# Small vectors loaded as one array, four token blocks requested first, the first tile's turned tokens copied by ScalarE alone

## The chip, the cores and the metric

The kernel runs on all 8 cores of one Trainium2 chip. Each core takes one of the eight sequences of the batch and works alone, with its own copy of all weights; nothing is exchanged between cores. The metric is device time in microseconds (us), of the slowest core. Engines are TensorE (PE), VectorE (DVE), ScalarE (ACT) and GpSimd (POOL); SyncE (SP) only issues DMAs here. POOL issues DMAs too: SP's travel on queue q1 and POOL's on queue q0, which also convert float32 to bf16 on the way.

## The reference

For `x` of shape (8, 2048, 1024), one layer of four parts, each added to `x` after a layer norm:

```
x = x + attn_a(layernorm(x))   # differential attention with normed q, k, 8 heads of 2 x 64
x = x + ffn(layernorm(x))      # one 1024x1024 matrix rounded to int4, plus a rank-16 term
x = x + attn_b(layernorm(x))   # causal attention with rotary positions, 16 heads of 64
x = x + ffn(layernorm(x))
```

What this case needs is the beginning of `attn_a`:

```
q, k, v = x @ Wq.T, x @ Wk.T, x @ Wv.T
cos_scale = 15 * sigmoid(cos_logit_scale_raw) * (1 + 0.5 * tanh(cos_head_delta - mean))
L1 = l2norm(q1) @ l2norm(k1).T * cos_scale       (L2 likewise from q2, k2)
G  = tanh(delta_gain * (L1 - L2))
lambda = exp(sum(lambda_q1 * lambda_k1)) - exp(sum(lambda_q2 * lambda_k2)) + 0.5
attn = softmax(L1 + G) - lambda * softmax(L2 - G)
y = rmsnorm(attn @ v) * subln_weight * 0.5
```

The small vectors are the four lambda vectors of 64, `cos_head_delta` and `delta_gain` of 8, `subln_weight` of 128, and one number, `cos_logit_scale_raw`.

## The kernel before, in words

Every engine's program is a list, written out in the order of the Python code; an engine runs its list in order and waits where a semaphore is named. A `Slot` counts the DMAs on one semaphore, and its token waits for all that were started on it so far. There is no scheduler for the part in question.

The tokens are 16 blocks of 128 rows, four blocks to a tile of 512. Stage 1 computes Q, K and V for all four tiles, in two pairs. A block b goes through these steps:

- `load_x1(b)` (SP): 512 KB into one of four buffers `x[:, b % 4]`. Block b + 4 is loaded when block b has been applied.
- `ln1_stats(b)`: two BATCH_NORM_STATS (L433) and one aggregate (L439) on DVE, then two tiny POOL operations (L189, L184) that make the reciprocal deviation.
- `ln1_apply(b)` (DVE, L191): the normed block, in bf16, into `wq[:, b % 8]`.
- `turn_pe(1)`: PE turns the block with the identity `c_ident` into two PSUM tiles, `pT0` and `pT1`, four matmuls each; ACT copies `pT0` (L175) and DVE casts `pT1` (L199) into `xn[t % 2]`. A PSUM tile is written again only when its copy is done.

At the beginning POOL issues `c_blk`, `c_ident`, then `w_q` in three pieces (columns 0 to 255, 256 to 511, 512 to 1023), `w_k` and `w_v` in two pieces each, and three small arrays. SP issues blocks 0 and 1 of x, the eight small vectors, each spread over 128 partitions by `bcast` (`wsub` has one number per partition), and blocks 2 and 3. Then the first four blocks are prepared, DVE in the order stats 0, stats 1, apply 0, stats 2, apply 1, stats 3, apply 2, apply 3, and turned.

Behind that DVE and ACT compute the scales of attention A out of the small vectors (`sc`, `gs`, `wsc`, `lam`, `cvec`, `lnc`), with two table loads on ACT. `group_qk` is one group: eight matmuls `pqk<-xn,w_q` of 128x512 for one head of one tile; it needs the four blocks of its tile and its piece of `w_q` (groups 0 and 1 the first, 2 and 3 the second, 4 to 7 the third). ACT squares the result, PE sums over 64 rows with `c_blk` (in `norm_of`, one group late), ACT takes logarithm and exponential, and DVE writes Q. The stage ends in a barrier of all engines; attention A, whose first matmul is `pD<-Qn,K`, begins after it.

Of the kernel before, what the change touches and what calls it, by code (L numbers as in the profile page):

```python
# [11 lines left out]
OP = mybir.AluOpType  # L12
# [8 lines left out]
HA = 8  # L21
HB = 16
LAMBDA_INIT = 0.5
# [163 lines left out]
def ts(q, out, a, s1, op0, s2=None, op1=None):  # L187
    if op1 is None:
        q.add(lambda e: e.tensor_scalar(out, a, s1, None, op0))  # L189
    else:  # L190
        q.add(lambda e: e.tensor_scalar(out, a, s1, s2, op0, op1))  # L191
# [6 lines left out]
def copy(q, out, in_):  # L198
    q.add(lambda e: e.tensor_copy(out, in_))  # L199
# [6 lines left out]
def _ap(t, offset, dims):  # L206
    return bass.AP(t.tensor if isinstance(t, bass.AP) else t, offset, dims)
# [50 lines left out]
def build_program():  # L258
# [3 lines left out]
    g = Prog(nc, base)  # L262
    pe, ve, ac, po, sy = g.all()

    di = {}

    def dram_in(name, shape):
        di[name] = nc.dram_tensor(name, list(shape), F32, kind="ExternalInput").ap()
# [2 lines left out]
    for w in ("WqT", "WkT", "WvT", "WoT", "WqB", "WkB", "WvB", "WoB", "fker"):  # L271
        dram_in(w, (NCH, 128, D))
    dram_in("bo", (D,))
    for w in ("lamq1", "lamk1", "lamq2", "lamk2"):
        dram_in(w, (64,))
    dram_in("dgain", (HA,))
    dram_in("chd", (HA,))
    dram_in("clsr", (1,))
    dram_in("wsub", (128,))
    dram_in("fbias", (D,))  # L280
    dram_in("fa", (NCH, 128, 16))
    dram_in("fb", (16, D))
# [9 lines left out]
    def sb(name, shape, dtype, stack=None):  # L292
        return (stack or base).enter_context(nc.sbuf_tensor(name, list(shape), dtype))
# [41 lines left out]
    wsc = sb("wsc", (128, 1), F32)  # L335
    lam = sb("lam", (128, 1), F32)
    gs = sb("gs", (128, HA), F32)
# [7 lines left out]

    sl_x = [Slot(g, f"d_x{i}") for i in range(4)]
    sl_w = [Slot(g, f"d_w{i}") for i in range(6)]
    sl_c = [Slot(g, f"d_c{i}") for i in range(3)]
    sl_o = Slot(g, "d_o")
    sl_f = Slot(g, "d_f")  # L350
    sl_wq = [Slot(g, f"d_wq{i}") for i in range(2)]
# [6 lines left out]
    W3 = [sb(f"w3_{n}", (128, NCH, D), BF16, s1) for n in "qkv"]  # L358
    blk = sb("c_blk", (128, 128), BF16, s1)
    ident = sb("c_ident", (128, 128), BF16, s1)  # L360
    sl_c[0].start(po, blk[:, :], di["blk"])
    c_tok = sl_c[0].start(po, ident[:, :], di["ident"])
    w_tok = []
    wq1_tok = []
    for k in range(2):
        w1_tok = sl_wq[k].start(po, W3[0][:, :, 256 * k:256 * (k + 1)],
                                w_cols(di["WqT"], 256 * k, 256))
        wq1_tok.append(w1_tok)
    for i, n in enumerate(("WqT", "WkT", "WvT")):
        for hf in range(2):  # L370
            if i == 0 and hf == 0:
                w_tok.append(w1_tok)
                continue
            w_tok.append(sl_w[2 * i + hf].start(
                po, W3[i][:, :, 512 * hf:512 * (hf + 1)], w_cols(di[n], 512 * hf, 512)))
# [3 lines left out]

    sc = sb("sc", (128, 400), F32, s1)  # L380

    def bcast(dst, name, n):
        return sl_c[1].start(sy, dst, _ap(di[name], 0, [[0, 128], [1, n]]))

    x_tok = {}

    def load_x1(b):
# [1 line left out]

    load_x1(0)  # L390
    load_x1(1)
    for i, n in enumerate(("lamq1", "lamk1", "lamq2", "lamk2")):
        bcast(sc[:, 64 * i:64 * (i + 1)], n, 64)
    bcast(sc[:, 256:264], "chd", HA)
    bcast(sc[:, 264:265], "clsr", 1)
    bcast(gs[:, :], "dgain", HA)
    s_tok = sl_c[1].start(sy, wsc[:, 0:1], di["wsub"])
    load_x1(2)
    load_x1(3)

# [73 lines left out]
    def turn_pe(n):  # L474

        for _ in range(n):
            b, a_tok = late_turn.popleft()
            t, tb = b // 4, b % 4
            toks = []
            pe.wait(a_tok)  # L480
            for k, q in enumerate((ac, ve)):
                pe.wait(pT_free[k])
                for c in range(4):
                    col = 128 * (4 * k + c)
                    mm(pe, pT[k][:, 128 * c:128 * (c + 1)], wq[:, b % 8, col:col + 128],
                       ident[:, :], True, True)
                q.wait(pe.done())
                out = xn[t % 2][:, 4 * k:4 * k + 4, 128 * tb:128 * (tb + 1)]
                if q is ac:
                    act(ac, out, blocks_of(pT[k][:, :], 4), AF.Copy)  # L490
                else:
                    copy(ve, out, blocks_of(pT[k][:, :], 4))
                pT_free[k] = q.done()
            xt[b] = (pT_free[0], pT_free[1])

    pqk_free = [None] * QK_BANKS
    pss_free = [None] * 2
# [6 lines left out]
    def norm_of(dst, t, h, bank, bi, p_tok, is_q):  # L504

        nonlocal n_nrm
        i = n_nrm % 2
        n_nrm += 1
        ac.wait(p_tok, sq_free[i])
        act(ac, sqb[i][:, :], bank[:, :], AF.Square)  # L510
        sq_tok = ac.done()

        def rest():
            pe.wait(sq_tok, pss_free[i])
            mm(pe, pss[i][:, :], blk[:, :], sqb[i][:, :], True, True)
            s_tok = pe.done()
            sq_free[i] = s_tok
            ac.wait(s_tok, rn_free[i])
            act(ac, rn[i][:, :], pss[i][:, :], AF.Ln, bias=lntiny)
            pss_free[i] = ac.done()  # L520
            ac.wait(pss_free[i])
            if is_q:
                act(ac, rn[i][:, :], rn[i][:, :], AF.Exp, scale=-0.5, bias=lnc[:, h:h + 1])
            else:
                act(ac, rn[i][:, :], rn[i][:, :], AF.Exp, scale=-0.5)
            ve.wait(ac.done())
            cap = c1e6[:, h:h + 1] if is_q else 1.0 / COS_EPS
            stt(ve, dst[:, h, QT * t:QT * (t + 1)], rn[i][:, :], cap, bank[:, :], OP.min, OP.mult)
            rn_free[i] = pqk_free[bi] = ve.done()

        late.append(rest)
# [107 lines left out]
    ve.add(lambda e: e.reduce_sum(sc[:, 270:271], sc[:, 0:64], AX))  # L639
    ve.add(lambda e: e.reduce_sum(sc[:, 271:272], sc[:, 128:192], AX))  # L640
    ts(ve, sc[:, 272:273], sc[:, 272:273], 1.0 / HA, OP.mult)
    ts(ve, gs[64:128, :], gs[64:128, :], -1.0, OP.mult)
    ts(ve, wsc[:, 0:1], wsc[:, 0:1], (1.0 - LAMBDA_INIT) * math.sqrt(128.0), OP.mult)
    ve.wait(ve.done())
    ts(ve, sc[:, 280:288], sc[:, 256:264], sc[:, 272:273], OP.subtract)
    ac.wait(ve.done())
# [478 lines left out]
    for s in range(-3, NS + NKS):  # L1125
        step_tanh(s + 2)
        step_exp(s)
        u, k = (s - NKS) // NKS, s % NKS
# [53 lines left out]
    pss_free = [y_evac[len(units) - 1]] * 2  # L1182
# [230 lines left out]
    for s in range(-2, NB + 5):  # L1413
        stepb_exp(s)
        stepb_Y(s - 2)
        if 0 <= s - 2 < NB:
            t, c, j = blocks[s - 2]
            if j == 4 * t + 3:
                i = t * (HB // 2) + c
                k = norm_b(t, c, i, s - 2)  # L1420
# [16 lines left out]
def _host_prep(inputs):  # L1437
    f = np.float32

    def rows(w):  # L1440
        return np.ascontiguousarray(w.reshape(NCH, 128, D))

    x = np.asarray(inputs["L0_attn_a_x"], f)
    com = {}
    for k, n in (("WqT", "Wq"), ("WkT", "Wk"), ("WvT", "Wv"), ("WoT", "Wo")):
        com[k] = rows(np.asarray(inputs["L0_attn_a_" + n], f).T)
    com["bo"] = np.asarray(inputs["L0_attn_a_bo"], f)
    com["lamq1"] = np.asarray(inputs["L0_attn_a_lambda_q1"], f)
    com["lamk1"] = np.asarray(inputs["L0_attn_a_lambda_k1"], f)
    com["lamq2"] = np.asarray(inputs["L0_attn_a_lambda_q2"], f)  # L1450
    com["lamk2"] = np.asarray(inputs["L0_attn_a_lambda_k2"], f)
    com["dgain"] = np.asarray(inputs["L0_attn_a_delta_gain"], f)
    com["chd"] = np.asarray(inputs["L0_attn_a_cos_head_delta"], f)
    com["clsr"] = np.asarray(inputs["L0_attn_a_cos_logit_scale_raw"], f).reshape(1)
    com["wsub"] = np.asarray(inputs["L0_attn_a_subln_weight"], f)
    wqkv = np.asarray(inputs["L0_attn_b_W_qkv"], f)
    for i, k in enumerate(("WqB", "WkB", "WvB")):
        com[k] = rows(wqkv[:, D * i:D * (i + 1)])
    com["WoB"] = rows(np.asarray(inputs["L0_attn_b_W_o"], f))
    com["fker"] = rows(np.asarray(inputs["L0_ffn_kernel"], f))  # L1460
    com["fbias"] = np.asarray(inputs["L0_ffn_bias"], f)
    com["fa"] = np.ascontiguousarray(np.asarray(inputs["L0_ffn_a"], f).reshape(8, 128, 16))
    com["fb"] = np.asarray(inputs["L0_ffn_b"], f)

    half = 32
    theta = 1.0 / (10000.0 ** (np.arange(half, dtype=np.float64) / half))
    ang = np.arange(T, dtype=np.float64)[:, None] * theta[None, :]
    cos_ = np.cos(ang).T.astype(f)
    sin_ = np.sin(ang).T.astype(f)
    com["cosb"] = np.ascontiguousarray(np.tile(cos_, (4, 1)))  # L1470
    sin_block = np.concatenate([-sin_, sin_], axis=0)
    com["sinbs"] = np.ascontiguousarray(np.tile(sin_block, (2, 1)))
    com["tri"] = np.ascontiguousarray(np.triu(np.ones((128, 128), f)))
    idx = np.arange(128)
    pm = np.zeros((128, 128), f)
    pm[idx ^ 32, idx] = 1.0
    com["perm"] = pm
    com["ident"] = np.ascontiguousarray(np.eye(128, dtype=f))
    com["blk"] = (idx[:, None] // 64 == idx[None, :] // 64).astype(f)

    in_maps = []
    for i in range(N_CORES):
        m = dict(com)
        m["xN"] = np.ascontiguousarray(x[i])
        in_maps.append(m)
    return in_maps
# [11 lines left out]
```

How the kernel before makes its waits and increments, by code:

```python
    def wait(self, *tokens):  # L57
        for tok in tokens:
            if tok is None:
                continue
            sem, val = tok
            if self.seen.get(sem.name, 0) >= val:
                continue
            self.seen[sem.name] = val
            self.ops.append([lambda e, s=sem, v=val: e.wait_ge(s, v), None, 0])
# [11 lines left out]
    def emit(self, engine):  # L77
        for fn, sem, k in self.ops:
            inst = fn(engine)
            if sem is not None:
                inst.then_inc(sem, k)
```

## Time and profile before

| | |
|---|---|
| runs of the kernel before | 1708.33, 1709.23, 1766.12 us (median 1709.23) |
| the profiled execution | 1708.93 us |
| its spans, first to last instruction | 1699.2 to 1706.4 us, the longest on core 3 |
| granted TensorE clock, mean of a core | 0.960 to 0.966 |
| PE busy (core of the page) | 1497.0 us, 88% |
| ACT busy | 1268.7 us, 74% |
| DVE busy | 1047.3 us, 61% |
| POOL busy | 532.5 us, 31% |
| DMA, mean over the span | 58 GB/s |

The span leaves out some 2.5 us around the first and the last instruction. A row of a timeline reads: start in us, busy time in us, engine, line, operation, output and input tiles, shapes, how many alike; in brackets how long the engine had been idle and what ended that. "SPq" is the SP queue issuing a DMA, and its time is that of the issue, not of the transfer. Merged rows with a count cover all that is alike, with what lies between them on other engines. Buffer numbers are left out of names.

### The profile page before, as it was taken

To read this page: it belongs to the slowest core of one execution; us is meant where nothing else is said; L and a number is where in the kernel's file an instruction comes from. 1 tells how busy PE (TensorE), PEld (TensorE's weight loads), DVE (VectorE), ACT (ScalarE), POOL (GpSimd) and SP (SyncE) were. 2 spreads that over 40 slices of the span, in tenths; PEclk is the share of its full clock that TensorE was granted. 3 is DMA by queue.
4 is the path that set the end of the run, shared out by engine and by line. 5 is a ranking of instruction groups with operands and counts; after the bars stand their busy time and mean duration, and the time that the engine had idled before them with its cause. 6 is when DMAs were issued, how large, how long until landed. Compare 5 with 4: busy or idle time off the path is not lost.

```text
span 1706.1 us, 40220 instructions; the slowest of 8 cores (1699.2 to 1706.4 us)
## 1 busy us (share of the span) xinstructions
PE 1497.0 (88%) x13132; PEld 787.9 (46%) x13344; DVE 1047.3 (61%) x1939; ACT 1268.7 (74%) x1904; POOL 532.5 (31%) x1089
## 2 busy tenths in 40 slices
PE   3899978789999999999999998759998899989987
PEld 1344434455555555555555555324443344444443
DVE  4474468878788787888878788432625454324215
ACT  2666649899999999999999999103234688878990
POOL 3010014444444444554444444522623000001001
PEclk9899989999999999999999999879997799989989
DMA  9614031211101111111111222473005222222303
GB/s 183 120 56 110 35 77 56 82 31 32 56 19 41 41 31 51 18 44 39 32 49 45 68 31 56 78 116 81 1 1 97 40 81 69 66 72 41 101 7 77
DMA packets 131468, 99.54 MB, mean 58 GB/s; under 512 B 99891, under 2 KB 115379, under 8 KB 131270
## 3 DMA queue, kind: packets, MB, share of 16 engines
q1 hardware_dynamic: 113910, 82.10, 18.0%
q0 software_dynamic: 17360, 14.88, 6.4%
q8 instruction: 115, 1.88, 0.5%
q14 instruction: 83, 0.68, 0.1%
HBM read 67.79 MB, written 20.97 MB: 52 GB/s over the span
## 4 chain that ended last, share of the span: by engine, by line
PE 41%; ACT 25%; issue 12%; DVE 5%; DMA 2%; POOL 0%; ACTq 0%; DVEq 0%; SPq 0%; POOLq 0%
ACT E L175 13%; PE pL L164 10%; ACT Gt L175 7%; PE pBb L164 6%; PE pY L171 5%; ACT EB L175 4%; PE pB L164 4%; PE pS L166 4%; PE pYb L171 4%; PE pL L166 3%; PE pD L164 3%; DVE Sx L184 2%; PE pS L164 1%; DMA xn<-xn 1%; PE pY L164 1%
## 5 line engine op out<-in xcount | busy, mean ns | idle before, releaser
L184 DVE TENSOR_TENSOR Sx<-pL,Gt 128x512 f32<-128x512 f32 x768 | 503.2, 685 | 138.3 <-PE pL L963 53.9
L175 ACT ACTIVATE E<-Sx 128x1024 bf16<-128x1024 f32 (+1 forms) x512 | 433.1, 846 | 15.4 <-DVE Sx L184 14.9
L175 ACT ACTIVATE EB<-pS,cst 128x1024 bf16<-128x1024 f32 (+1 forms) x320 | 296.5, 988 | 66.6 <-PE pS L166 63.7
L171 PE MATMUL pY<-V,E 128*128 128x129 bf16 x4096 | 308.2, 221 | 23.9 <-ACT E L175 11.7
L175 ACT ACTIVATE Gt<-pD 128x512 bf16<-128x512 f32 x512 | 306.4, 598 | 24.4 <-PE pD L164 15.4
L171 PEld LDWEIGHTS pY<-V,E 128*128 128x128 bf16 x4096 | 259.7, 98 | 92.7 <-issue 40.3
L166 PE MATMUL pL<-Q,K 64*128 64x256 bf16 x1536 | 198.8, 274 | 23.8 <-ACT E L175 15.8
L164 PE MATMUL pD<-Qn,K 128*128 128x256 bf16 x1024 | 196.4, 273 | 23.1 <-ACT Gt L175 15.8
L189 POOL TENSOR_SCALAR st<-st 128x1 f32<-128x1 f32 x64 | 17.8, 278 | 502.9 <-DVE st L439 486.3
L175 ACT ACTIVATE E<-pL 128x512 bf16<-128x512 f32 x256 | 154.1, 602 | 6.0 <-PE pL L171 0.5
L166 PE MATMUL pS<-Q,K 64*128 64x512 bf16 (+3 forms) x640 | 123.4, 379 | 21.8 <-ACT EB L175 15.7
L171 PE MATMUL pYb<-V,EB 128*128 128x65 bf16 x2176 | 134.3, 202 | 4.7 <-DVE ytb L184 4.5
L175 ACT ACTIVATE qb<-pL 128x512 bf16<-128x512 f32 x64 | 38.2, 597 | 128.0 <-PE pL L164 125.5
L171 PEld LDWEIGHTS pYb<-V,EB 128*128 128x128 bf16 x2176 | 91.6, 101 | 76.8 <-issue 70.6
L166 PEld LDWEIGHTS pL<-Q,K 64*128 64x128 bf16 x1536 | 60.7, 94 | 139.6 <-issue 139.6
L184 POOL TENSOR_TENSOR cu<-Yt,cst 128x2 f32<-128x2 f32 x64 | 44.1, 688 | 228.6 <-DVE Yt L199 228.4
L184 DVE TENSOR_TENSOR EB<-EB,c_tri 128x256 bf16<-128x256 bf16 x128 | 36.5, 290 | 123.7 <-ACT EB L175 122.8
L963 PE MATMUL pL<-Q,K 64*128 64x256 bf16 x512 | 100.2, 276 | 0.0
L164 PEld LDWEIGHTS pD<-Qn,K 128*128 128x128 bf16 x1024 | 75.4, 97 | 45.3 <-issue 39.3
L433 DVE BATCH_NORM_STATS2 st<-x 128x6 f32<-128x512 f32 x128 | 86.3, 685 | 13.8 <-DMA x<-xN 11.2
L164 PE MATMUL pB<-Wo,Q 128*128 128x512 bf16 x240 | 71.7, 384 | 19.0 <-DMA Q<-yt 11.3
L184 DVE TENSOR_TENSOR ro<-pL,x 128x512 f32<-128x512 f32 x64 | 43.6, 682 | 64.6 <-ACT qb L175 64.4
(165 smaller groups left out, 2167.8 us busy)
## 6 DMA issues: line engine op xcount, KB each, us to landing
x<-xN SPq DMA_DIRECT2D x32, 512.0 KB, 5.2
x<-x SPq DMA_DIRECT2D x32, 512.0 KB, 3.3
out<-x SPq DMA_DIRECT2D x16, 512.0 KB, 2.8
x<-fker SPq DMA_DIRECT2D x3, 2048.0 KB
x<-WoT SPq DMA_DIRECT2D x2, 2048.0 KB
xn<-xn SPq DMA_DIRECT2D x16, 256.0 KB, 2.1
w_k<-WkT POOLq DMA_DIRECT2D x2, 1024.0 KB, 40.7
w_v<-WvT POOLq DMA_DIRECT2D x2, 1024.0 KB, 58.2
```

Source lines behind the costliest of these rows:

```text
L164: q.add(lambda e: e.matmul(out, lhsT, rhs, start=start, stop=stop))
L166: q.add(lambda e: e.matmul(out, lhsT, rhs, start=start, stop=stop, tile_position=pos))
L171: q.add(lambda e: e.matmul(out, lhsT, rhs, start=first, stop=last, skip_group_check=True))
L175: q.add(lambda e: e.activation(out, in_, func, **kw))
L184: q.add(lambda e: e.tensor_tensor(out, a, b, op))
L189: q.add(lambda e: e.tensor_scalar(out, a, s1, None, op0))
L433: ve.add(lambda e: e.bn_stats(st[:, b, 6 * half:6 * half + 6], x[:, b % 4, 512 * half:512 * (half + 1)]))
L963: pe.add(lambda e, s=s, cs=cs, js=js, h=h, qsl=qsl, jj=jj: e.matmul(pL[2 * (s % 2) + 1][:, cs], K[64:128, h, js], Q[64:128, h, qsl], start ...
```

## The change

Three edits. The eight small vectors are laid out by the host code as one array `small` of 128 x 329 float32, already repeated over the partitions, and one DMA brings it to `sc`, between blocks 1 and 2 of x. `gs` and `wsc` were loaded directly before; now a DVE copy and the two multiplies that were there fill them from `sc`. `c_blk` moves on POOL from the first place to behind the first two pieces of `w_q`, on a slot of its own, and PE waits for it where it first reads it. For the first four blocks both PSUM tiles of turned tokens are copied by ACT.

```diff
-    for w in ("lamq1", "lamk1", "lamq2", "lamk2"):
-        dram_in(w, (64,))
-    dram_in("dgain", (HA,))
-    dram_in("chd", (HA,))
-    dram_in("clsr", (1,))
-    dram_in("wsub", (128,))
+    dram_in("small", (128, 329))
...
-    sl_c[0].start(po, blk[:, :], di["blk"])
     c_tok = sl_c[0].start(po, ident[:, :], di["ident"])
...
         wq1_tok.append(w1_tok)
+    blk_tok = sl_c[3].start(po, blk[:, :], di["blk"])
...
     load_x1(0)
     load_x1(1)
-    for i, n in enumerate(("lamq1", "lamk1", "lamq2", "lamk2")):
-        bcast(sc[:, 64 * i:64 * (i + 1)], n, 64)
-    bcast(sc[:, 256:264], "chd", HA)
-    bcast(sc[:, 264:265], "clsr", 1)
-    bcast(gs[:, :], "dgain", HA)
-    s_tok = sl_c[1].start(sy, wsc[:, 0:1], di["wsub"])
+    s_tok = sl_c[1].start(sy, sc[:, 0:329], di["small"])
     load_x1(2)
     load_x1(3)
...
-            for k, q in enumerate((ac, ve)):
+            for k, q in enumerate((ac, ac if b < 4 else ve)):
...
-            pe.wait(sq_tok, pss_free[i])
+            pe.wait(sq_tok, pss_free[i], blk_tok)
...
-    ts(ve, gs[64:128, :], gs[64:128, :], -1.0, OP.mult)
-    ts(ve, wsc[:, 0:1], wsc[:, 0:1], (1.0 - LAMBDA_INIT) * math.sqrt(128.0), OP.mult)
+    copy(ve, gs[0:64, :], sc[0:64, 320:328])
+    ts(ve, gs[64:128, :], sc[64:128, 320:328], -1.0, OP.mult)
+    ts(ve, wsc[:, 0:1], sc[:, 328:329], (1.0 - LAMBDA_INIT) * math.sqrt(128.0), OP.mult)
```

How the instructions stand on SP at the beginning of the program, before (`x` are the token blocks, `sc`, `gs` and `wsc` the small vectors):

```order
L120 DMA x<-xN 128x1024 x2
L120 DMA sc<-lamq 128x64
L120 DMA sc<-lamk 128x64
L120 DMA sc<-lamq 128x64
L120 DMA sc<-lamk 128x64
L120 DMA sc<-chd 128x8
L120 DMA sc<-clsr 128x1
L120 DMA gs<-dgain 128x8
L120 DMA wsc<-wsub 128x1
L120 DMA x<-xN 128x1024 x14
```

And with the change:

```order
L103 UNCONDITIONAL_BRANCH
L120 DMA x<-xN 128x1024 x2
L120 DMA sc<-small 128x329
L120 DMA x<-xN 128x1024 x14
L127 DMA_TRANSPOSE xn<-wq 128x8x128 x8
```

Eight loads between the second and the third block have become one. On ACT, from the first table load to the first square of a group, before (`pT` are the turned tokens in PSUM, `xn` where they go):

```order
L413 ACT_TABLE_LOAD
L175 ACTIVATE xn<-pT 128x4x128 x4
L633 ACT_TABLE_LOAD
L175 ACTIVATE sc<-sc 128x2
L175 ACTIVATE sc<-sc 128x8
L175 ACTIVATE sc<-sc 128x1
L665 ACT_TABLE_LOAD
L175 ACTIVATE lnc<-cvec,cst 128x8
```

And with the change (the numbers behind the tiles are those of the buffers; all lines of the file have moved up by 13 there):

```order
L400 ACT_TABLE_LOAD
L175 ACTIVATE xn0<-pT0 128x4x128
L175 ACTIVATE xn0<-pT1 128x4x128
L175 ACTIVATE xn0<-pT0 128x4x128
L175 ACTIVATE xn0<-pT1 128x4x128
L175 ACTIVATE xn0<-pT0 128x4x128
L175 ACTIVATE xn0<-pT1 128x4x128
L175 ACTIVATE xn0<-pT0 128x4x128
L175 ACTIVATE xn0<-pT1 128x4x128
L620 ACT_TABLE_LOAD
L175 ACTIVATE sc<-sc 128x2
```

Four copies have become eight, ahead of the second table load. On DVE the four casts that stood between the apply of block 3 and the scales are gone, and one copy of 64x8 is added among the scales. On POOL `c_blk` has moved from the first place of the loads to the fourth.

## Rows read from the trace of the kernel before

**Rows 1.** The page, its part on the chain that ended last, by line.

```profile
ACT E L175 13%; PE pL L164 10%; ACT Gt L175 7%; PE pBb L164 6%; PE pY L171 5%; ACT EB L175 4%; PE pB L164 4%; PE pS L166 4%; PE pYb L171 4%; PE pL L166 3%; PE pD L164 3%; DVE Sx L184 2%; PE pS L164 1%; DMA xn<-xn 1%; PE pY L164 1%
```

**Rows 2.** The view of the cores: span and mean granted clock.

```profile
core 2: 1699.2 us, clock 0.966
core 3: 1706.4 us, clock 0.966
core 4: 1706.1 us, clock 0.960
```

**Rows 3.** Timelines of cores 2, 3, 4 and 5: the first projection matmuls.

```profile
28.69 5.08 PE L164 MATMUL pqk<-xn,w_q 128*128 128x512 bf16 x16 [0.94 <-DVE xn L199]
...
35.76 5.09 PE L164 MATMUL pqk<-xn,w_q 128*128 128x512 bf16 x16 [0.94 <-DVE xn L199]
...
32.10 5.56 PE L164 MATMUL pqk<-xn,w_q 128*128 128x512 bf16 x16 [0.94 <-DVE xn L199]
...
33.81 6.37 PE L164 MATMUL pqk<-xn,w_q 128*128 128x512 bf16 x16 [0.94 <-DVE xn L199]
```

**Rows 4.** Timelines of cores 2, 3, 4 and 5: attention A's first matmul.

```profile
232.49 0.59 PE L164 MATMUL pD<-Qn,K 128*128 128x256 bf16 x2 [7.14 <-POOLq L65]
...
238.97 0.59 PE L164 MATMUL pD<-Qn,K 128*128 128x256 bf16 x2 [7.14 <-POOLq L65]
...
236.60 0.59 PE L164 MATMUL pD<-Qn,K 128*128 128x256 bf16 x2 [7.14 <-POOLq L65]
...
237.22 0.58 PE L164 MATMUL pD<-Qn,K 128*128 128x256 bf16 x2 [7.16 <-POOLq L65]
```

**Rows 5.** Timeline, SP's issues: two of core 3, then one of core 5.

```profile
4.33 8.22 SPq L120 DMA_DIRECT2D sc<-clsr  x1
...
15.21 39.52 SPq L120 DMA_DIRECT2D x<-xN  x10
...
9.42 19.47 SPq L120 DMA_DIRECT2D x<-xN  x6
```

**Rows 6.** Timeline, DVE: three rows of core 3, then two of core 5.

```profile
24.19 1.28 DVE L433 BATCH_NORM_STATS2 st<-x 128x6 f32<-128x512 f32 x2 [11.23 <-DMA x<-xN]
...
29.62 0.81 DVE L191 TENSOR_SCALAR wq<-x,st 128x1024 bf16<-128x1024 f32 x1 [0.90 <-POOL st L184]
...
34.92 0.69 DVE L199 CAST xn<-pT 128x512 bf16<-128x512 f32 x1 [0.84 <-PE pT L164]
...
8.18 1.29 DVE L433 BATCH_NORM_STATS2 st<-x 128x6 f32<-128x512 f32 x2 [0.69 <-DMA x<-xN]
...
22.25 1.29 DVE L433 BATCH_NORM_STATS2 st<-x 128x6 f32<-128x512 f32 x2 [9.29 <-DMA x<-xN]
```

**Rows 7.** Timeline of core 3: block 0's apply and its first copy.

```profile
12.15 0.81 DVE L191 TENSOR_SCALAR wq<-x,st 128x1024 bf16<-128x1024 f32 x1 [3.50 <-POOL st L184]
...
13.79 0.60 ACT L175 ACTIVATE xn<-pT 128x512 bf16<-128x512 f32 x1 [10.65 <-PE pT L164]
```

**Rows 8.** Core 3: windows 10:15; DMA queues at 16:18, then 20:25 (packets, MB, share).

```profile
10.00:15.00 5.00, 1.01 (x8) 0.77 (x8) 0.81 (x1) 0.60 (x1) 3.09 (x6) 1.00 0.08 10
...
q0 software_dynamic: 577, 0.30, 122.0%
...
q1 hardware_dynamic: 554, 1.07, 77.4%
q0 software_dynamic: 555, 0.28, 43.5%
```

**Rows 9.** Tile w_q, its three loads from issue to landing: core 2, core 3.

```profile
DMA to landing us min/median/max: 11.6/17.6/29.4
...
DMA to landing us min/median/max: 17.6/25.0/35.8
```

**Rows 10.** Timeline of core 3: the fifth group, and DVE's write of Q after it.

```profile
45.89 1.89 PE L164 MATMUL pqk<-xn,w_q 128*128 128x512 bf16 x8
...
52.52 0.74 DVE L195 SCALAR_TENSOR_TENSOR Q<-rn,c1e,pqk 128x512 bf16<-128x512 f32 x1
```

More of the change, by code:

```diff
@@ L347, in build_program @@
     sl_w = [Slot(g, f"d_w{i}") for i in range(6)]
-    sl_c = [Slot(g, f"d_c{i}") for i in range(3)]
+    sl_c = [Slot(g, f"d_c{i}") for i in range(4)]
     sl_o = Slot(g, "d_o")
@@ L380, in build_program @@
     sc = sb("sc", (128, 400), F32, s1)
-    def bcast(dst, name, n):
-        return sl_c[1].start(sy, dst, _ap(di[name], 0, [[0, 128], [1, n]]))
     x_tok = {}
@@ L1447, in _host_prep @@
     com["bo"] = np.asarray(inputs["L0_attn_a_bo"], f)
[L1448 to L1455, printed above, removed]
+    small = np.zeros((128, 329), f)
+    for k, n in enumerate(("lambda_q1", "lambda_k1", "lambda_q2", "lambda_k2")):
+        small[:, 64 * k:64 * (k + 1)] = np.asarray(inputs["L0_attn_a_" + n], f).reshape(1, 64)
+    small[:, 256:264] = np.asarray(inputs["L0_attn_a_cos_head_delta"], f).reshape(1, HA)
+    small[:, 264] = np.asarray(inputs["L0_attn_a_cos_logit_scale_raw"], f).reshape(1)
+    small[:, 320:328] = np.asarray(inputs["L0_attn_a_delta_gain"], f).reshape(1, HA)
+    small[:, 328] = np.asarray(inputs["L0_attn_a_subln_weight"], f)
+    com["small"] = small
     wqkv = np.asarray(inputs["L0_attn_b_W_qkv"], f)
```

## The prediction

> **What bounds the kernel now.** I read three views in this order. First the chain of waits: it runs almost wholly through the attention stages, named there by their tiles (E, Gt, pL, pY, EB) [rows 1]. The change touches none of them; what it can change is when they begin. Second, the spans of the cores, which differ by 7 us [rows 2]. Third, the timelines of single cores, where the cores have run the experiment already. The first projection matmul starts at 28.69 us on core 2, 32.10 on core 4, 33.81 on core 5 and 35.76 on core 3 [rows 3]. Attention A's first matmul starts at 232.49, 236.60, 237.22 and 238.97 [rows 4], that is 203.8, 204.5, 203.4 and 203.2 us later. From there to the end of cores 2, 4 and 3 it is 1466.7, 1469.5 and 1467.4 us [rows 2, 4]. So a late first projection is carried to the end nearly one for one, with 1 to 2 us of scatter. Call its start T1. Over all eight cores, span less T1 runs from 1670.5 (core 2) to 1674.0 us (core 4).
>
> What sets T1? On core 3 the SP queue has issued seven loads by 4.33 us, two of x and five small ones; the next small one holds the queue for 8.22 us, two more follow, and block 2 of x is asked for only at 15.21 [rows 5]. VectorE (DVE) begins on it at 24.19, after 11.23 us of waiting for that load [rows 6]. Asking earlier is not enough: core 5 issues block 2 at 9.42 and has it only at 22.25 [rows 5, 6], because it moves behind the small pieces on the same queue. After that comes a fixed run of work: the apply of block 3 starts 5.43 us after block 2's statistics, the last cast of turned tokens ends at 35.61, and T1 is 0.15 later [rows 3, 6].
>
> **Part 1, the small vectors as one load.** Removed on SP are eight loads, 1024 pieces of 4 to 256 bytes; added is one with 128 pieces of 1316 bytes. Block 2 of x is then the fourth load of the queue and block 3 the fifth, and seven loads were issued by 4.33. Block 1, the second, has landed by 8.18 on core 5 [rows 6]. A block costs 1.07 MB in 5 us, 2.45 us for its 0.5 MB, while weights move beside it [rows 8]. The new small load has no row: it costs between nothing, hidden between blocks, and a block's 2.45; I take 1, nearer the low end, since its pieces are a third of a block's 4096 bytes. Block 2 is then in at about 8.2 + 1 + 2.45 = 11.6, block 3 at 14.1. DVE waits for neither: it applies block 0 at 12.15 to 12.96, because POOL issues its own loads until 11 us and computes the deviations after them [rows 7]. Core 5 has the same (22.25 - 9.29 = 12.96) [rows 6]. POOL's order stays but for c_blk, so DVE starts block 2 at 12.96 and, by the same spacing, the apply of block 3 at 12.96 + 5.43 = 18.39. At the dearer end of the small load, 2.45, block 2 would be in at 13.1 and T1 0.1 later.
>
> **Part 2, the first tile's copies on ScalarE (ACT).** Removed: four DVE casts. All of them stand behind the apply of block 3 on DVE and chain through one PSUM tile, so that from that apply (29.62) to T1 pass 6.14 us [rows 3, 6]. Added: four ACT copies of 0.60 us. An apply is followed by ACT's first copy after 13.79 - 12.15 = 1.64 us [rows 7]. Block 3: copies from 18.39 + 1.64 = 20.03 and from 20.63, ended at 21.23, and T1 = 21.4. ACT is free then: block 2's two copies come 1.7 us sooner, as its apply does, and take 1.2. Behind the copies ACT has a table load and three tiny activations, which still come right after T1; I cost them at nothing, because they are as far behind it as now. If ACT fell behind by one or two copies, 0.6 to 1.2 us would show. DVE gets one more copy of 64 x 8 elements, under 0.2 us, beside ACT's copies; uncovered it costs just that.
>
> **Part 3, c_blk behind two pieces of w_q.** One small load less ahead of the weights. Its first reader comes some 6 us after T1, at 27; the piece ahead of it lands at 20 to 29 us on cores 2 and 3 (25.0 and 17.6 from an issue at 3.8) [rows 9]. So it is free unless the weights are late, which is rival A.
>
> **PE's clock.** The turns now run densely just before T1, and still the first 16 projection matmuls take 5.09 us on core 3 and 6.37 on core 5 [rows 3], against 1.89 for 8 later on [rows 10]: the first of them run at the lower level, 1.2 GHz. Core 5's slower start is gone by attention A (203.4 us, next to 203.2) [rows 3, 4]. With the turns spread over 8 us the low level may last longer, by these rows 0 to 1.3 us. I take 0, the value of core 5. The Trainium skill, "TensorE: Matmul & The Clock Gate", section "What's actually happening", has the half rate as the default that sustained activity releases; by that alone all 16 would run at it, an estimate of 6.8 us, and the sum would be 1.7 us longer. The trace agrees on the two levels, not on the loss.
>
> **The sum.** T1 moves to 21.4 on every core, so the slowest core will be the one with the longest rest: 21.4 + 1674.0 = 1695.4 us against 1706.4 now, 11.0 less. Core 3 gains 14.4, but is no longer the slowest. The profiled execution took 1708.93, so **1697.9 us**; it stands 0.3 below the median of the runs, 1709.23. About 2%, 34 us, is what a measurement of this kernel can tell from no change; the forecast lies within it.
>
> **Rivals.**
> A. *The weights become the bound.* The fifth group needs w_q's third piece 10.13 us after T1 (45.89) [rows 3, 10], from now on at 31.5. There are about 2 us in hand, since DVE is held up there by other work: its write of Q at 52.52 comes 6.6 us after that group starts. So PE may wait until 33.5 for nothing. The piece, issued at 4.7, landed at 34.1 on core 2 and 40.5 on core 3 [rows 9]. What now? Alone the weights move 0.30 MB in 2 us, beside x loads 0.28 in 5, as many packets as x's queue [rows 8]. The 2 MB of w_q cost 13.6 us, and six x blocks of 2.45 us beside them 6 x 2.45 x (1 - 0.056 / 0.15) = 9.2: from a start at about 7 us this ends at 29.8. The other end is core 2's 34.1. I take 32, in time. The rival has it later, because blocks 2 to 7 of x all ask ahead of it: each us past 33.5 costs one, up to 7.0 with core 3's 40.5; the middle gives 1701.4. 20%. The skill's "DMA: Bandwidth & Descriptors", section "Queues, rings and completion order", has each DMA engine take turns between queues by packets; the equal counts of rows 8 agree.
> B. *The DMA's idle time is not the small pieces' doing.* On core 3 DMA is busy 0.08 of its time between 10 and 15 us [rows 8]. If that comes from all cores loading at once, block 2 lands late as on core 2, where T1 less core 3's 11.57 (35.76 - 24.19) puts it at 17.1: 4.1 later, 1702. Against it: nothing but tiny pieces was queued on SP then. 11%.
> C. *Slower.* The third piece lands after 33.5 + 11.0 = 44.5 us; then more is lost than won. The software queue would have to starve through the whole first tile. At 49 the time is 1697.9 + 15.5 = 1713. Its share beside x in rows 8 speaks against it. 3%.
> D. *The start is won and given back* at a wait fixed in time before attention A: 1704 to 1709. The four cores of rows 3 and 4 speak against it. 8%.
> The forecast keeps 58%; its own range is 1695 to 1700.
>
> **Numbers.** 1694 to 1704 holds the forecast and nearly all of A and B; outside lie C, D and a rest of A, together under 2 in 10. Faster by over 2%: 1%; within 2%: 98%; slower by over 2%: 1%, a starvation well beyond C.
>
> **What would show it.** In the new trace: one small load on SP and four x loads issued by 4 us; statistics of block 2 at 13 us with no wait for a DMA; eight ACT copies, the last ended at 21.2; T1 at 21.4 on all cores, with little spread; no wait ahead of the fifth group; attention A from 224.6 to 225.9. A wait of PE for a DMA between 27 and 36 us would show A; statistics of block 2 after 15 us B; attention A starting at 230 or later with T1 at 21.4 D.

## The result, and the profile after

The changed kernel takes 1698.39 us (median of 4 runs, 1696.79 to 1699.01). Against the kernel before the ratio is 0.993, with a 95% interval of 0.9907 to 0.9954. The forecast was 1697.9 us, from the profiled execution's 1708.93; the profiled execution of the change took 1698.39. In a later comparison the ratio was 0.9933 (0.9919 to 0.9948). Runs that the chip disturbed are left out of ratios, so where a median below looks out of line with its ratio, the ratio counts.

The spans of three cores, the shortest, the second longest and the longest, and their clocks; they answer to [rows 2]:

```profile
core 1: 1689.4 us, clock 0.969
core 2: 1694.8 us, clock 0.961
core 7: 1695.3 us, clock 0.963
```

Longest was 1695.4 in the forecast and is 1695.3. The beginning on core 7, rows picked out of a timeline of SP, DVE, ACT and PE, against [rows 3, 5 to 7]:

```profile
1.98 0.43 SPq L120 DMA_DIRECT2D sc<-small  x1
2.45 38.00 SPq L120 DMA_DIRECT2D x<-xN  x10
...
12.17 0.81 DVE L191 TENSOR_SCALAR wq<-x,st 128x1024 bf16<-128x1024 f32 x1 [3.38 <-POOL st L184]
12.90 1.28 DVE L420 BATCH_NORM_STATS2 st<-x 128x6 f32<-128x512 f32 x2
...
18.32 0.81 DVE L191 TENSOR_SCALAR wq<-x,st 128x1024 bf16<-128x1024 f32 x1 [0.90 <-POOL st L184]
...
20.06 1.08 ACT L175 ACTIVATE xn<-pT 128x512 bf16<-128x512 f32 x2 [0.63 <-PE pT L164]
...
21.29 5.21 PE L164 MATMUL pqk<-xn,w_q 128*128 128x512 bf16 x16 [0.90 <-ACT xn L175]
27.53 0.38 PE L164 MATMUL pss<-sqb,c_blk 128*128 128x512 bf16 x1 [1.02 <-ACT sqb L175]
```

Read from the top: block 2 of x is asked for at 2.45 instead of 15.21 us; the apply of block 0 waits for POOL as before, at 12.17; the statistics of block 2 follow at 12.90 with no bracket, so nothing was waited for, where 11.23 us of waiting stood. The last copy ends at 21.14 and T1 is 21.29 (the forecast had 21.4). All eight cores have T1 between 21.28 and 21.32; before they lay between 28.69 and 35.76.

The fifth group, and the first matmul of attention A, on cores 7 and 2 for the group and cores 7 and 1 for attention A:

```profile
32.22 1.89 PE L164 MATMUL pqk<-xn,w_q 128*128 128x512 bf16 x8 [0.42 <-DMA w_q<-WqT]
...
34.31 3.48 PE L164 MATMUL pqk<-xn,w_q 128*128 128x512 bf16 x8 [2.51 <-DMA w_q<-WqT]
...
225.63 0.59 PE L164 MATMUL pD<-Qn,K 128*128 128x256 bf16 x2 [7.14 <-POOLq L65]
...
221.41 0.58 PE L164 MATMUL pD<-Qn,K 128*128 128x256 bf16 x2 [7.15 <-POOLq L65]
```

The group does wait for w_q now, 0.4 to 2.5 us (on core 3 the view names DVE for a wait of 1.46, but the piece landed only 0.2 us before the group started). Before no core showed such a wait. In the mean of the eight cores the group starts at 33.5 us, and attention A at 223.8, where it started at 236.3 before. The windows of the engines on core 7 between 10 and 15 us (the last numbers are the granted clock, the DMA's busy share and GB/s), and the two queues between 20 and 25:

```profile
10.00:15.00 5.00, 1.01 (x8) 0.78 (x8) 2.73 (x5) 1.08 (x2) 3.46 (x7) 1.00 1.21 183
```

```profile
q1 hardware_dynamic: 271, 0.99, 58.8%
q0 software_dynamic: 294, 0.28, 44.4%
```

[rows 8] are core 3's, with a busy share of 0.08 and 10 GB/s between 10 and 15 us; core 3 has 1.25 and 208 GB/s there now, and core 7, which had 0.85 and 109 GB/s, has 1.21 and 183. So the idle stretch went with the small pieces, as the forecast had it. Beside x loads the weights still move 0.28 MB in 5 us; the two queues moved 271 and 294 packets. That they take turns by packets is what the Trainium skill has in "DMA: Bandwidth & Descriptors", section "Queues, rings and completion order"; these nearly equal counts agree.

### The profile page after: what moved, and what is told of

Its sections match the earlier page's. It is cut to its first block, busy times and chain, and to the rows that moved or that the text cites. A ratio compares the mean times of both kernels' runs of the same rounds, so it can differ in the third digit from the quotient of the medians.

```text
span 1694.8 us, 40429 instructions; the slowest of 8 cores (1689.4 to 1695.3 us)
## 1 busy us (share of the span) xinstructions
PE 1527.1 (90%) x13344; PEld 787.2 (46%) x13344; DVE 1045.2 (62%) x1936; ACT 1271.2 (75%) x1908; POOL 533.7 (31%) x1089
## 4 chain that ended last, share of the span: by engine, by line
PE 44%; ACT 23%; issue 12%; DVE 4%; DMA 2%; POOL 1%; ACTq 0%; DVEq 0%; POOLq 0%; SPq 0%
ACT E L175 12%; PE pL L164 9%; ACT Gt L175 7%; PE pY L171 7%; PE pBb L164 6%; PE pB L164 4%; PE pS L166 4%; ACT EB L175 4%; PE pYb L171 4%; PE pL L166 4%; PE pD L164 3%; PE pS L164 1%; DVE Sx L184 1%; DMA xn<-xn 1%; PE pL L171 1%
## 5 line engine op out<-in xcount | busy, mean ns | idle before, releaser
L175 ACT ACTIVATE E<-Sx 128x1024 bf16<-128x1024 f32 (+1 forms) x512 | 433.2, 846 | 15.2 <-DVE Sx L184 14.4
L164 PE MATMUL pD<-Qn,K 128*128 128x256 bf16 x1024 | 196.3, 273 | 19.9 <-ACT Gt L175 12.5
L184 POOL TENSOR_TENSOR cu<-Yt,cst 128x2 f32<-128x2 f32 x64 | 44.2, 690 | 227.4 <-DVE Yt L199 227.2
L171 PE MATMUL pL<-Gt,nident 128*128 128x512 bf16 x256 | 100.2, 391 | 0.0
```

The costliest lines, as they stand in the source:

```text
L164: q.add(lambda e: e.matmul(out, lhsT, rhs, start=start, stop=stop))
L171: q.add(lambda e: e.matmul(out, lhsT, rhs, start=first, stop=last, skip_group_check=True))
L175: q.add(lambda e: e.activation(out, in_, func, **kw))
L184: q.add(lambda e: e.tensor_tensor(out, a, b, op))
```

## The experiments

The theory is the prediction's: T1 sets the time, nearly one for one, as long as the weights are there ("start theory"). It has to answer for three edits, so each was tried alone or left out. Beside the times the text gives the mean start of attention A over the eight cores of the profiled execution. It shows what reached the end of this stage, and the rest of the program varies on its own: from attention A to the end the mean is 1467.8 to 1469.7 us in the traces of this case.

**What a comparison can tell.** The kernel before against itself, and the change once more; no edit in either.

> The kernel before, unchanged, measured against itself. It shows what a comparison of this kernel can tell from no change. If the bound of 2% that the prediction used is right, the interval of the ratio is near 0.98 to 1.02; if the start theory can be tested at all, it is within 0.3% of 1: about 0.997 to 1.003, and a change of 0.7% is no longer no change.

> The changed kernel, unchanged, beside the others of this call. Start theory: ratio 0.993 to 0.995, 1698 to 1700 us; T1 21.3 us on every core, the fifth group starts at 32 to 34.5. If the first result was luck: ratio above 0.997.

Measured: 1.0007 (0.9994 to 1.002) and 0.9933 (0.9919 to 0.9948); medians 1708.7 and 1698.66 us. A comparison of this kernel tells 0.2 to 0.3% from no change, and the change's 0.7% is well outside. In the second trace of the change T1 is 21.3 us on seven cores and 22.3 on one, and attention A starts at 224.1 in the mean.

**The one load without the copies.**

```diff
-            for k, q in enumerate((ac, ac if b < 4 else ve)):
+            for k, q in enumerate((ac, ve)):
```

> The changed kernel, but with the first tile's turned tokens copied by ScalarE and VectorE in halves as before. Start theory (what the first projection matmul gains, T1, is carried to the end): the casts stand behind the apply of block 3 again, so T1 is 18.3 + 6.1 = 24.5 us on all cores instead of 21.3; time 3.1 to 3.3 above the changed kernel's 1698.4, about 1701.6, ratio to before 0.995. Rival (the third piece of w_q, landed at 32 to 34 us, is what starts the fifth group anyway, so the copies bought nothing): T1 24.5, but the time stays at 1698.4.

Measured: 0.9948 (0.9926 to 0.9969), 1700.93 us. T1 is 24.45 to 24.48 on all cores. On core 4, the last cast, the first group and the sixth turn:

```profile
23.64 0.69 DVE L199 CAST xn<-pT 128x512 bf16<-128x512 f32 x1 [0.84 <-PE pT L164]
24.48 5.83 PE L164 MATMUL pqk<-xn,w_q 128*128 128x512 bf16 x16 [0.94 <-DVE xn L199]
...
43.98 0.58 PE L164 MATMUL pT<-c_ident,wq 128*128 128x128 bf16 x4 [4.18 <-DVE xn L199]
```

No core waits for w_q in this run, and still the time is 2.3 to 2.5 us above the change's 1698.39 and 1698.66. The reason stands in the last row. A turn of the second tile waits for a cast on DVE, and it starts 19.5 us after T1, here at 43.98 and in the changed kernel at 40.80; the fifth group's lateness disappears in the idle time ahead of it. The intervals of the two ratios overlap; what parts them are the times that the ratios count, 1700.5 to 1701.1 us here and 1696.7 to 1699.4 for the changed kernel. Attention A starts at 229.0 in the mean, 5.2 us later than in the changed kernel. So the rival, for which the copies bought nothing, is out. The start theory asked for 3.1 to 3.3 us and got 2.4 in the time; where the difference between the 5.2 at attention A and the 2.4 at the end goes, no run shows.

**The copies alone.** The kernel before with

```diff
-            for k, q in enumerate((ac, ve)):
+            for k, q in enumerate((ac, ac if b < 4 else ve)):
```

> The kernel before with one edit: the first tile's eight copies all on ScalarE; small loads and order as before. Start theory: from the apply of block 3 to T1 3.0 us instead of 6.1, so T1 is 25.5 to 32.6 on the cores (block 2 still lands at 17 to 24), 3.1 earlier each; time 3.1 below before, about 1705.8, ratio 0.998. Rival (the copies only matter once the loads are early, since VectorE has idle time while it waits for block 2): no change, T1 as before.

Measured: 0.9991 (0.9976 to 1.0007), 1708.76 us beside 1709.56. On core 4, block 2's statistics and T1:

```profile
21.10 1.29 DVE L433 BATCH_NORM_STATS2 st<-x 128x6 f32<-128x512 f32 x2 [8.14 <-DMA x<-xN]
...
29.51 5.80 PE L164 MATMUL pqk<-xn,w_q 128*128 128x512 bf16 x16 [0.90 <-ACT xn L175]
```

From one to the other it is 8.41 us where [rows 3, 6] have 35.76 - 24.19 = 11.57. So the 3.1 us are taken from T1 here too, on every core (28.21 to 30.84). The time does not show it clearly: the interval holds both the expected 0.998 and 1. As a time this run is inconclusive. Attention A starts at 233.5 us in the mean, 2.8 earlier than in the trace before, so the gain did get that far; the rival said that T1 would stay, and that is out.

**The order alone.** The kernel before, still with eight small loads, but blocks 2 and 3 ahead of them.

```diff
     load_x1(0)
     load_x1(1)
+    load_x1(2)
+    load_x1(3)
     for i, n in enumerate(("lamq1", "lamk1", "lamq2", "lamk2")):
...
     s_tok = sl_c[1].start(sy, wsc[:, 0:1], di["wsub"])
-    load_x1(2)
-    load_x1(3)
```

> The kernel before with one edit: x blocks 2 and 3 are issued ahead of the eight small loads, which stay eight. Rival 1 (order is all, the small pieces cost only what waits behind them): T1 24.5 us as in the run with one load and split copies, time about 1701.6, ratio 0.995. Rival 2 (the 1024 small pieces hold up both queues wherever they stand): the DMA is nearly idle for some 6 us later on, VectorE waits for the small vectors after the casts (to 26 us or more) or x blocks 4 and 5 come late; time 1704 to 1708.

Measured: 0.9941 (0.9924 to 0.9959), 1700.18 us. That can't be told from the single load (0.9948) with the same copies, and attention A starts at 228.2 us in the mean, where the single load has 229.0. T1 is 24.41 to 24.44. But the small pieces have not become harmless. Core 5's first turn, then core 0's windows from 15 to 20 us and its waits for w_q:

```profile
13.60 1.01 PE L164 MATMUL pT<-c_ident,wq 128*128 128x128 bf16 x8 [13.60 <-DMA c_ident<-ident]
```

```profile
15.00:20.00 5.00, 0.75 (x6) 0.55 (x7) 3.68 (x7) 0.60 (x1) 2.00 (x4) 1.00 0.72 70
```

```profile
34.07 1.67 PE L164 MATMUL pqk<-xn,w_q 128*128 128x512 bf16 x7 [3.21 <-DMA w_q<-WqT]
41.50 2.71 PE L164 MATMUL pqk<-xn,w_q 128*128 128x512 bf16 x8 [3.60 <-DMA w_q<-WqT]
```

DMA moves 70 GB/s there (224 on the same core in the changed kernel), the identity lands just after it is wanted, and on core 0 the third and the fifth group wait over 3 us. Core 0 was the slowest of that execution (1699.7 us, next 1697.7). So both rivals were right in part: the mechanism of the second is there, its price of 1704 to 1708 is not. The sixth turn starts at 43.7 to 48.6 us on the cores, against 43.9 to 44.2 with the single load, so a part of those waits fits into idle time.

**c_blk first again.** The changed kernel with `c_blk` issued ahead of `c_ident`, on its own slot.

```diff
+    blk_tok = sl_c[3].start(po, blk[:, :], di["blk"])
     c_tok = sl_c[0].start(po, ident[:, :], di["ident"])
...
-    blk_tok = sl_c[3].start(po, blk[:, :], di["blk"])
```

> The changed kernel with c_blk issued first on POOL again, as before the change. Start theory: T1 stays 21.3; the pieces of w_q land 0 to 0.5 us later, the fifth group may be late to 34.8 for nothing; the time is that of the changed kernel, 1698 to 1699, ratio 0.9935. Rival (one small load ahead of the weights costs as much as the SP ones did): 1701.

Measured: 0.9932 (0.9919 to 0.9945), 1698.1 us; T1 21.27 to 21.29 on seven cores and 21.86 on one. The third edit is worth nothing that can be measured. But `c_blk` lands at 21.7 to 27.0 us in the changed kernel, where it landed at 8.2 to 10.0 here, and its first reader stands at 27.5: the margin is half a us on the worst core.

**The weights late.** The changed kernel with the third piece of w_q issued behind the first half of w_k.

```diff
-    for i, n in enumerate(("WqT", "WkT", "WvT")):
+    w_tok = [w1_tok] + [None] * 5
+    for i, hf, n in ((1, 0, "WkT"), (0, 1, "WqT"), (1, 1, "WkT"), (2, 0, "WvT"), (2, 1, "WvT")):
```

> The changed kernel with the third piece of w_q issued behind the first half of w_k instead of ahead of it. Its landing goes from 32 to 34 us to 39 to 43. In-hand theory (PE may wait for it until 33.5 us for nothing, then each us costs one): T1 stays 21.3, PE waits 8 to 11 us ahead of the fifth group, time 6 to 9 us above the changed kernel, 1704 to 1708. Rival (the weights are not near the bound, other idle time absorbs it): below 1700.

Measured: 0.9996 (0.9984 to 1.0009), 1710.14 us. Core 5's and core 7's fifth group:

```profile
44.32 3.57 PE L164 MATMUL pqk<-xn,w_q 128*128 128x512 bf16 x8 [12.51 <-DMA w_q<-WqT]
```

```profile
46.44 3.57 PE L164 MATMUL pqk<-xn,w_q 128*128 128x512 bf16 x8 [14.58 <-DMA w_q<-WqT]
```

T1 is still 21.3, and all that the change gained is gone. The group starts at 44.9 us in the mean of the cores, and the ratio is 0.63% above the change's 0.9933, which is 10.8 us. If each us past some point costs one, that point is about 44.9 - 10.8 = 34.1, to some 3 us by the intervals of the ratios. The traces say the same more closely: the group starts 11.4 us later than in the changed kernel and attention A 11.0 (234.8 us in the mean). After the long wait the group itself ran at the half clock, 1.2 GHz, on every core (3.46 to 3.57 us instead of 1.89), so a part of the 11.0 is the clock's and not the transfer's. The forecast had 33.5 for that point and 44.5 for the one where the change breaks even. The size came out above what was expected here, 10.8 us instead of 6 to 9, because PE waited 12.1 to 14.6 us and not 8 to 11: the piece landed later than 39 to 43.

**POOL's deviations first.** The changed kernel, with w_k, w_v and three small arrays issued behind the first four blocks' deviations.

```diff
-    for i, n in enumerate(("WqT", "WkT", "WvT")):
-        for hf in range(2):
...
+    w_tok.append(w1_tok)
+    w_tok.append(sl_w[1].start(po, W3[0][:, :, 512:1024], w_cols(di["WqT"], 512, 512)))
...
     ln1_apply(3)
+    for i, n in ((1, "WkT"), (2, "WvT")):
+        for hf in range(2):
+            w_tok.append(sl_w[2 * i + hf].start(
+                po, W3[i][:, :, 512 * hf:512 * (hf + 1)], w_cols(di[n], 512 * hf, 512)))
...
     turn_pe(4)
```

> The changed kernel, but POOL computes the deviations of the first four blocks ahead of its issues of w_k, w_v and the three small arrays, so the apply of block 0 no longer waits for POOL until 12.15 us. Start theory: block 0 applied at 8 to 9, block 2 lands at 11, T1 at 19.5 to 20; the sixth turn comes 19.5 us after T1, at 39.2, and the time is 1.5 us below the changed kernel's of this call. Rival (the weights have become the bound: the fifth group starts at 32 to 34.5 wherever T1 is, and what it may be late for nothing shrinks with T1, to about 33): the same time as the changed kernel, or up to 1 us more.

Measured: 0.9933 (0.9919 to 0.9948), the very ratio of the change beside it. The 1.5 us of the start theory would be 0.09%, which lies within that interval, so the time alone doesn't decide. On core 4, the apply of block 0, T1, the fifth group and the sixth turn:

```profile
9.39 0.80 DVE L191 TENSOR_SCALAR wq<-x,st 128x1024 bf16<-128x1024 f32 x1
...
20.30 6.33 PE L164 MATMUL pqk<-xn,w_q 128*128 128x512 bf16 x16 [0.90 <-ACT xn L175]
...
34.53 1.89 PE L164 MATMUL pqk<-xn,w_q 128*128 128x512 bf16 x8 [3.63 <-DMA w_q<-WqT]
...
40.90 0.38 PE L164 MATMUL pT<-c_ident,wq 128*128 128x128 bf16 x4 [1.30 <-DVE xn L199]
```

Block 0 was applied at 8.1 to 9.7 us. T1 came forward by a mean of 1 us (19.43 to 22.03), and not to the 19.5 to 20 expected: DVE now waits for block 2, and starts on it at 11.0 to 13.6. The fifth group (32.9 to 34.9, mean 33.8) didn't come forward at all, and attention A starts at 223.4 us in the mean, beside 223.8 and 224.1 in the two traces of the change. The last row says why. The sixth turn stands 20.6 us after T1 here, not 19.5; it is tied to the fifth group instead, 6.4 us behind it. With a fifth group at the half clock (cores 0, 2, 5 and 6, 3.4 to 3.6 us) that distance is 8.1 to 8.3. So the start theory ends here and the rival holds: with T1 at 20 to 21 us the landing of w_q's third piece holds the sixth turn on most cores. The mechanism was named in the prediction as rival A.

**The second tile's copies on ACT too,** twice.

```diff
-            for k, q in enumerate((ac, ac if b < 4 else ve)):
+            for k, q in enumerate((ac, ac if b < 8 else ve)):
```

> The changed kernel, with the second tile's turned tokens also copied by ScalarE alone. In the changed kernel PE waits 2 to 3.5 us ahead of the sixth turn and 2 to 2.6 ahead of the ninth group for a cast that stands behind an apply on VectorE. Theory (that cast is what bounds the first tile): the sixth turn starts at 37 to 38 instead of 40.8, attention A 2 to 3 us earlier, time 1.5 to 3 us less. Rival (ScalarE is the bound there: its three activations of a group take 2.0 us and four copies add 2.4): the same time within 1 us.

> The changed kernel with the second tile's copies on ScalarE as well, again, as the measure for the next two. Ratio 0.990 to 0.993, about 1696; attention A from 220 to 223.6.

Measured: 0.9916 (0.9898 to 0.9934) and 0.9908 (0.9894 to 0.9922), 1696.06 and 1693.83 us. Core 0, the sixth turn and the ninth group:

```profile
37.69 0.87 PE L164 MATMUL pT<-c_ident,wq 128*128 128x128 bf16 x8 [0.19 <-ACT xn L175]
...
46.72 3.38 PE L164 MATMUL pqk<-xn,w_q 128*128 128x512 bf16 x8 [2.46 <-ACT xn L175]
```

The turn has come forward from 40.8 to 37.7 us on this core, and to 37.1 to 39.1 on five of the eight; on the three whose fifth group ran at the half clock (3.2 to 3.5 us) it stands at 40.4 to 41.0. The ninth group waits for a copy on ACT now, but at 46.1 to 50.0, where the change has 49.0 to 50.7. Attention A starts at 221.2 and 221.4 us in the mean of the two runs, 2.6 earlier than in the change, with the fifth group where it was. So the theory that the cast behind an apply bounds the first tile holds, and the weights and the cast bound it together: the turn waits for whichever comes last.

**Both, and w_q in four pieces.** Two kernels. The first joins the two edits just shown; the second also splits the piece that the fifth group waits for:

```diff
-    w_tok.append(sl_w[1].start(po, W3[0][:, :, 512:1024], w_cols(di["WqT"], 512, 512)))
+    for k in range(2):
+        wq1_tok.append(sl_w[k].start(po, W3[0][:, :, 512 + 256 * k:768 + 256 * k],
+                                     w_cols(di["WqT"], 512 + 256 * k, 256)))
+    w_tok.append(wq1_tok[3])
...
-        if is_q and h < 4:
+        if is_q:
```

> POOL's deviations ahead of its later DMA issues, and both tiles' copies on ScalarE. T1 19.5 to 22. Weights theory: nothing is left for the fifth group to be late for, but it still starts at 33 to 34.8 when the third piece of w_q has landed, so the time equals that of the kernel with the two tiles' copies alone, within 1 us. Rival (the start theory alone, every us of T1 counts once the casts are gone): 1 to 1.7 us less than that.

> As the kernel before it, and w_q in four pieces of 256 columns instead of two and one of 512, so that the fifth group waits only for the third quarter. Weights theory: that quarter lands 3 us before the whole piece, at 29.5 to 31.5, the fifth group starts by 31.5, the time is 2 to 3 us below the kernel without the split, about 1693.5. Rival (ScalarE is the bound of the first tile by now): the fifth group starts earlier, attention A doesn't, same time within 1 us.

Measured: both, without the split, 0.9929 (0.9896 to 0.9961); with it 0.9893 (0.9879 to 0.9907), 1691.56 us. The first has too wide an interval to be told by its time from the second tile's copies alone (0.9908). Its trace has T1 at 20.5 us in the mean, 0.8 earlier, and attention A at 221.5, no earlier than their 221.4: as the weights theory has it. On core 5 of the second, T1, the fifth group and the ninth:

```profile
20.75 6.39 PE L164 MATMUL pqk<-xn,w_q 128*128 128x512 bf16 x16 [0.90 <-ACT xn L175]
...
31.17 1.89 PE L164 MATMUL pqk<-xn,w_q 128*128 128x512 bf16 x8
...
44.90 1.89 PE L164 MATMUL pqk<-xn,w_q 128*128 128x512 bf16 x8 [2.47 <-ACT xn L175]
```

The fifth group has no bracket any more: it waits for nothing. Attention A starts at 217.7 to 219.3 us on the cores, where the change has 221.4 to 225.6; the mean, 218.6, is 2.9 earlier than without the split. This version beats the kernel before and the changed one, by 1.07% and, ratio over ratio, by 0.40%.

## Why the prediction was right or wrong

**The number and the mechanism held.** 1697.9 against 1698.39 us, and the steps are found in the trace where they were put: block 2 no longer waited for, block 0's apply held by POOL at 12.17, T1 at 21.28 to 21.32 on all cores. That the longest span came out at 1695.3 for 1695.4 is partly luck. The sum took the longest rest from T1 to the end, 1674.0 us, from core 4, as if a core kept its own. Core 4's fell to 1671.1, and core 7's rose from 1671.1 to 1674.0; over the four executions of the result the longest span is 1694.5 to 1696.3.

**The step that failed is the one on what a measurement tells.** The prediction said that "about 2%, 34 us, is what a measurement of this kernel can tell from no change; the forecast lies within it", and put 98% on "within 2%", which by that sentence is no change. No row stood behind the 2%. What the runs showed in its place: the kernel against itself gives 1.0007 (0.9994 to 1.002), and the change measured 0.993 with an interval of 0.9907 to 0.9954, which leaves no room for no change. A forecast of 0.993 was a forecast of a faster kernel, and it should have been said so. The row for it was at hand: the first two times of the table, 1708.33 and 1709.23, lie 0.05% apart. By a bound of 0.3%, 5 us, the prediction's own cases read: the forecast, A and B are faster (58, 20 and 11%), D is mostly no change and C slower.

**Part 1, the single load.** The time came from the order, as the argument had it (block 2 moves behind the small pieces). Eight loads behind the x blocks did as well as one. The new load has landed 8.6 to 10.8 us into the execution. Block 2 landed 3.2 to 4.5 us after block 1, at 10.4 to 12.5 (the forecast had 11.6), and DVE was ready for it at 12.9. Less the 2.45 us of a block that leaves 0.8 to 2.0 for the new load, where the term was 1; its upper end, 2.45, would hardly have mattered.

**Part 2, the copies.** 3.1 us of T1, seen in both runs that isolate them; 2.4 us of time on top of the early loads, and too little to be told from nothing without them. I had written that ACT is ready, and it was: in the changed kernel it stood idle 0.6 to 1.2 us before each later pair of copies (waits of 1.24, 1.13 and 0.63 us for the turn's tile).

**Part 3, c_blk.** Free in the changed kernel, as said, but with little to spare. In one trace of the second tile's copies it landed at 28.3 us and PE waited 1.33 us for it. With POOL's deviations first, where T1 is earlier, such a wait stands on one core (0.98), on four of the joined kernel (up to 2.14) and on three of the one with four pieces (up to 1.56). Issued first it lands by 10 us and costs nothing that was measured; those later kernels were not tried that way.

**PE's clock.** I took 0 and the runs agree. The first 16 matmuls took 4.89 to 6.44 us on the cores, yet the `pss` matmul behind them, which waits for ACT on four of the cores, starts at 27.53 to 27.59 on all. So 1.5 us of difference in the burst come to 0.06 behind it. The Trainium skill's default of a half clock ("TensorE: Matmul & The Clock Gate", section "What's actually happening") gave an estimate of 6.8 us for the burst, with all 16 matmuls at it and no release. No core took that long, so on every core the clock rose within the burst; and had it not, the burst would have ended at 28.1, which is half a us past the `pss` matmul's start and not 1.7.

**Rival A was nearer than I gave it.** The forecast had no wait ahead of the fifth group, and named a wait of PE for a DMA between 27 and 36 us as A's sign. The sign is there: the third piece of w_q landed at 32.0 to 34.1 us (32 was forecast, and core 2's 34.1 as the other end), and PE waited up to 2.51 us. A's price, 1701.4, is not, for by the late-weights run the free time ends at about 34.1. It ends sooner where the wait brings on the half clock: on cores 2 and 6 the fifth group started at 34.31 and 33.90 and took 3.48 and 3.56 us, and the sixth turn stands at 42.28 and 41.95, 0.9 us or more behind the 40.8 to 41.1 of the other six. The change stops at the very point where the weights take over, which the run with POOL's deviations first then shows. In A's sum 2 MB at 0.15 MB a us are 13.3 us (14.0 for the full 2.1 MB) and not 13.6, which changes nothing.

**Rival B is out**: with eight cores loading, core 3's DMA is busy 1.25 between 10 and 15 us, where it had 0.08. The idle time does depend on what the other cores do, though, as the last section shows. **C and D** did not come; the late-weights run put C's mechanism to the test, with its break-even in the right place (44.5 forecast; at a mean of 44.9 the ratio is 0.9996).

**The spread between cores** is what is left. The forecast put attention A at 224.6 to 225.9 us and it starts at 221.4 to 225.6. From T1 to attention A it is 200.1 us on core 1 and 204.3 on core 7, at the same T1. The windows of core 1, then of core 7, from 36 to 46 and 46 to 56 us (the third number from the end is the granted clock):

```profile
36.00:46.00 10.00, 7.56 (x51) 3.67 (x48) 6.53 (x12) 7.21 (x14) 1.51 (x3) 1.00 1.07 253
46.00:56.00 10.00, 7.41 (x39) 3.46 (x38) 3.35 (x5) 6.63 (x12) 0.00 (x0) 1.00 1.13 186
```

```profile
36.00:46.00 10.00, 6.29 (x34) 3.04 (x32) 5.63 (x10) 4.81 (x9) 1.45 (x3) 0.83 1.07 246
46.00:56.00 10.00, 7.14 (x31) 2.97 (x30) 3.44 (x5) 4.87 (x9) 0.00 (x0) 0.83 1.14 190
```

And the sixth turn on core 1 and on core 7:

```profile
40.86 0.38 PE L164 MATMUL pT<-c_ident,wq 128*128 128x128 bf16 x4 [2.14 <-DVE xn L199]
```

```profile
40.80 0.38 PE L164 MATMUL pT<-c_ident,wq 128*128 128x128 bf16 x4 [3.52 <-DVE xn L199]
```

The turn comes at the same time on both. Core 1 has waited 1.85 us for w_q before, stands idle for only 2.14 us here and keeps 2.4 GHz; core 7 waited 0.42, stands idle for 3.52 and drops to 1.2 GHz twice. The other cores fit in between. In these two windows the granted clock is below 1.00 never on core 1 (attention A at 221.4), once on cores 0, 3 and 4 (223.0 to 223.3), and twice on cores 2, 5, 6 and 7 (224.5 to 225.6). So the spread goes with the clock. That a wait ahead of the fifth group can help in this way is read from these rows; no run isolates it. On cores 2 and 6 the wait itself ended in a fifth group at the low level, and the length of a wait doesn't settle it: ahead of the ninth group cores 1 and 3 both stand idle for 2.01 us, core 1 keeps 2.4 GHz and core 3's group takes 2.83 us.

## What to carry to other kernels

Ask for the large loads that the first tile needs before the small ones, and look for the time in when a load lands, not in when it is issued: what moves ahead of it on its queue counts. A core-to-core spread at the beginning is an experiment already made; if the starts are carried to the ends, a start saved is a time saved, until the next transfer (here a piece of the first weight) is the one that comes last, and then a split of that piece is worth more than an earlier start (2.9 us at attention A against 0.4). A start that comes earlier also uses up the slack of what was moved back because it had time, as `c_blk` here. Before you call a forecast "no change", take from repeated times of the same kernel how small a change a comparison can show.

## What the hardware did that I had not expected

Eight loads with 1024 pieces of 4 to 256 bytes, 0.14 MB in all, left the DMA busy 0.08 of the time for 5 us on core 3. The weights on the other queue stood still with them (18 packets, 0.01 MB, from 10 to 15 us), although POOL had issued them from 2.9 us on; with the small loads gone DMA was busy 1.25 in the same window.

This doesn't happen on every core, and it comes in pairs. From 8 to 11 us, before, cores 0, 3, 4 and 7 have a busy share of 0.08 to 0.22 and 9 to 16 GB/s, and cores 1, 2, 5 and 6 have 0.95 to 1.30 and 123 to 168 GB/s. In the other trace of the same kernel the slow ones are 1, 2, 4 and 6 (0.16 to 0.36, against 0.51 to 1.06), and in that of the copies alone 1, 3, 5 and 7 (0.16 to 0.25, against 0.87 to 1.01). In all three it is one core of each pair (0 and 1, 2 and 3, 4 and 5, 6 and 7), and which one changes from execution to execution. That points to something that a core shares with its neighbour, though no run tests it. SP comes to issue block 2 at 11.5 to 15.2 us on the four slow cores of the first trace and at 8.3 to 9.4 on the others, yet T1 is hardly later for it (31.04 to 35.76 against 28.69 to 33.81), since on the others the block moves behind the small pieces. What the pair shares, and why the other queue stops as well, stays open: no run separates the number of pieces from their being spread copies of the same few bytes, and none loads on one core alone.
